# A state-space layer with a routed feed-forward on one core: the first chunk's first block spread over partitions by TensorE instead of through DRAM

## What is computed

```python
xn = layernorm(x)                         # over the 256 features
u_inner = xn @ W_in.T + b_in              # 1024 columns: x (512 channels) and z (the gate)
dbc = x @ W_x.T + b_x                     # 16 columns of delta_raw, 16 of B, 16 of C
delta = softplus(delta_raw @ W_dt.T + b_dt)
A = -exp(A_log)                           # 512 channels x 16 states
h = h * exp(delta_t * A) + x_t * delta_t * B_t      # for each token t in turn
y_t = sum over states of h * C_t
out = (y + x * D) * silu(z) @ W_out.T + b_out
```

## Time and profile before

| | before |
|---|---|
| median of 3 runs | 1965.87 us (1964.99 to 1971.97) |
| the profiled execution | 1968.13 us, of which 1966.3 us are the span from first to last instruction |
| VectorE busy | 1823.1 us, 93% of the span |
| GpSimd busy | 1791.7 us, 91% |
| TensorE busy (matmul) | 1628.6 us, 83% |
| ScalarE busy | 1431.6 us, 73% |
| DMA | 234.92 MB, 119 GB/s on average |
| first scan of VectorE starts | 59.62 us |

### The profile page before, as it was taken

One profiled execution on the slowest core, in us unless ns is written; L12 is line 12 of the kernel. 1 busy time (PEld: TensorE's weight loads), 2 busy tenths in 40 slices (PEclk: granted clock), 3 DMA queues, 4 the chain that ended last, 5 costly groups with the idle time before them and its releaser, 6 DMA issues.

```text
span 1966.3 us, 25727 instructions
## 1 busy us (share of the span) xinstructions
PE 1628.6 (83%) x6816; PEld 808.6 (41%) x6816; DVE 1823.1 (93%) x2246; ACT 1431.6 (73%) x2755; POOL 1791.7 (91%) x780
## 2 busy tenths in 40 slices
PE   3364779898898989889898988889898898988899
PEld 1111224444443444444344444444444444444456
DVE  2799999999999999999999999999999999999951
ACT  3566767877787777878777787877778787777643
POOL 1899999999999999999999999999999999999920
PEclk8666879999899999989999999999999999999999
DMA  4646553544646365464636536463643646265200
GB/s 167 142 112 155 119 138 90 142 123 92 161 111 155 91 152 123 96 151 112 161 84 149 126 92 152 112 165 79 158 118 94 148 111 166 68 156 118 58 14 19
DMA packets 146761, 234.92 MB, mean 119 GB/s; under 512 B 22064, under 2 KB 46896, under 8 KB 146096
## 3 DMA queue, kind: packets, MB, share of 16 engines
q1 hardware_dynamic: 146608, 233.18, 48.7%
HBM read 190.11 MB, written 42.99 MB: 119 GB/s over the span
## 4 chain that ended last, share of the span: by engine, by line
DVE 32%; POOL 23%; issue 17%; PE 17%; ACT 5%; DMA 1%; DVEq 0%; SPq 0%; POOLq 0%; ACTq 0%
POOL hs L1344 14%; DVE decay L1286 13%; DVE hs L1276 8%; DVE hs L1286 7%; POOL hs L1356 6%; PE bank L910 4%; PE bank L932 4%; ACT decay L1089 2%; PE y_ps L946 2%; POOL e_dt L1334 1%; DVE st L1146 1%; POOL z_dt L1323 1%; PE bank L894 1%; PE bank L914 1%; PE bank L884 1%
## 5 line engine op out<-in xcount | busy, mean ns | idle before, releaser
L1344 POOL TENSOR_TENSOR hs<-dx_rep,b_rep 128x2048 f32<-128x2048 f32 x256 | 1161.8, 4541 | 13.4 <-issue 11.1
L1286 DVE TENSOR_TENSOR_SCAN decay<-decay,state,hs 128x512 f32<-128x512 f32 x640 | 796.2, 1277 | 34.2 <-ACT decay L1089 27.4
L1089 ACT ACTIVATE decay<-dt_rep,a_sb 128x512 f32<-128x512 f32 x1024 | 690.0, 685 | 28.7 <-DMA dt_rep<-rep_scratch 10.3
L1286 DVE TENSOR_TENSOR_SCAN hs<-decay,state,hs 128x512 f32<-128x512 f32 x384 | 487.3, 1269 | 4.3 <-ACT decay L1089 3.7
L1356 POOL TENSOR_TENSOR hs<-hs,c_rep 128x1024 f32<-128x1024 f32 x192 | 453.6, 2362 | 6.3 <-ACT state L1103 6.3
L1276 DVE TENSOR_TENSOR hs<-decay,c_rep 128x1024 f32<-128x1024 f32 x320 | 385.1, 1204 | 0.0
L946 PE MATMUL y_ps<-hs,nsum 128*32 128x512 f32 x2048 | 290.3, 641 | 48.8 <-POOL hs L1356 30.6
L910 PE MATMUL bank<-w_i_sb,x_t 128*128 128x512 f32 x484 | 273.5, 693 | 28.9 <-DVE silu L1174 25.5
L868 PE MATMUL bank<-xn_t,w_in_sb 128*128 128x512 f32 x512 | 258.5, 635 | 14.5 <-ACT x_t L996 4.9
L1103 ACT COPY state<-decay 128x2 f32<-128x2 f32 x320 | 51.0, 159 | 266.8 <-DVE hs L1276 260.1
L932 PE MATMUL bank<-w_o_sb,r_t 128*128 128x256 f32 x944 | 224.1, 392 | 2.6 <-ACT r_t L1074 1.8
(11 more groups left out here) (163 smaller groups left out, 1747.7 us busy)
## 6 DMA issues: line engine op xcount, KB each, us to landing
dx_rep<-rep_scratch SPq DMA_DIRECT2D x256, 256.0 KB, 4.7
dt_rep<-rep_scratch SPq DMA_DIRECT2D x256, 256.0 KB, 7.6
b_rep<-bc_scratch SPq DMA_DIRECT2D x256, 64.0 KB, 3.9
rep_scratch<-z_dt SPq DMA_DIRECT2D x64, 256.0 KB, 2.5
rep_scratch<-e_dt SPq DMA_DIRECT2D x64, 256.0 KB, 2.7
c_rep<-bc_scratch SPq DMA_DIRECT2D x256, 64.0 KB, 2.6
xin<-in_u SPq DMA_DIRECT2D x16, 512.0 KB, 4.2
xr<-in_u SPq DMA_DIRECT2D x16, 512.0 KB, 4.3
```

Of the source, the lines that this page charges most:

```text
L1089: nc.scalar.activation(decay[:, j, :], dt_rep[m % 2][:, j, :], ACT.Exp, scale=a_sb[:, J * s + j:J * s + j + 1]).then_inc(decay_ready, 1)
L1286: v.tensor_tensor_scan(hs[s % 4][:, j, :] if kept else decay[:, j, :], decay[:, j, :], hs[s % 4][:, j, :], state[:, b, n:n + 1], ALU.mult, ...
L1344: nc.gpsimd.tensor_tensor(hs[s % 4][:], dx_rep[m % 2][:], b_rep[:, k, :].unsqueeze(1).to_broadcast([P, J, T]), ALU.mult).then_inc(input_re ...
```

## The change

Nothing is changed from chunk 0's second block on. For its first block, and in the prologue:

1. TensorE spreads `e_dt` and `z_dt` of block 0: 4 matmuls for each of 4 tiles j, for each of the two, into `decay` (PSUM), each with 32 columns of the identity as its weights and 32 output partitions. ScalarE copies the first four tiles to `dt_rep[0]`, VectorE the other four to `dx_rep[0]`.
2. The Exp and Ln of the first two blocks are done one block at a time (`first_block` on ScalarE), and V and U of both on VectorE (`first_step`), which also makes the first product with B, in halves; GpSimd only counts it as done.
3. TensorE multiplies zeros: 14 matmuls of 256 columns from the start, and 4 more behind D 1.
4. ScalarE makes the inverse root ahead of A; `rates` (Exp and multiplication of `a_sb`) stands behind the copies.
5. SP no longer loads block 0 back; it issues four groups of B and C ahead of the store, and stores block 1 ahead of block 0.
6. VectorE's work on the later loads stands ahead of job C's part.

```diff
+FIRST = dict(SIDE, pool=[[[x for x in part if x not in ("V0 pre", "U0 pre")] for part in row] for row in SIDE["pool"]])
...
-                for i in range(2):
+                for i in (1, 0) if isinstance(c, int) and c == 0 and pair == 0 else range(2):
                     for kind, src in ((1, z_dt), (0, e_dt)):
                         sp.dma_start(rep_dram[kind, 2 * pair + i], src[:, i, :]).then_inc(rep_stored[2 * pair + i], 16)
...
+                if "main" not in parts and "pre" in parts:
+
+                    waits((bc_stored, 32))
+                    for which, k in ((0, 0), (0, 1), (1, 0), (0, 2)):
+                        load_bc(which, k)
+                    store_rep(0, 0)
+                    for which, k in ((0, 3), (1, 1), (1, 2)):
+                        load_bc(which, k)
...
+            def warm(turns):
+
+                for _ in range(turns):
+                    pe.matmul(y_ps[:, 0:256], state[:].rearrange("p b n -> p (b n)")[:, 0:P],
+                              state[:].rearrange("p b n -> p (b n)"), start=True, stop=True)
+
+            def spread_first():
+
+                for kind, ready, src in ((0, first_delta, e_dt), (1, first_dx, z_dt)):
+                    pe.wait_ge(ready, 1)
+                    for j in range(J):
+                        if kind == 1:
+                            pe.wait_ge(dt_loaded[0], 16 * (j + 1))
+                        for n in range(4):
+                            mm = pe.matmul(decay[32 * n:32 * n + 32, j, :], ident[:, 32 * j:32 * j + 32], src[:, 0, :],
+                                           start=True, stop=True)
+                        mm.then_inc(first_filled, 1)
+
+            pe.wait_ge(zeroed, 1)
+            warm(WARM)
             wait_first(pe)
...
+                    if isinstance(c, int) and c < 0 and i == 1:
+                        mm.then_inc(filled[b], 1)
+                        warm(4)
+                        spread_first()
+                        return
...
-            wait_first(act)
-            nc.scalar.activation(a_sb[:], a_sb[:], ACT.Exp).then_inc(a_ready, 1)
-            act.wait_ge(a_ready, 1)
-            nc.scalar.mul(a_sb[:], a_sb[:], -1.0).then_inc(a_ready, 1)
-            act.wait_ge(a_ready, 2)
+            def rates():
+
+                nc.scalar.activation(a_sb[:], a_sb[:], ACT.Exp).then_inc(a_ready, 1)
+                act.wait_ge(a_ready, 1)
+                nc.scalar.mul(a_sb[:], a_sb[:], -1.0).then_inc(a_ready, 1)
+                act.wait_ge(a_ready, 2)
+
+            def first_block():
+
+                wait_read(act, -1, "pre", "D", (0,))
+                nc.scalar.activation(e_dt[:, 0, :], e_dt[:, 0, :], ACT.Exp, scale=-1.0).then_inc(first_exp, 1)
+                act.wait_ge(first_exp, 1)
+                nc.scalar.activation(e_dt[:, 0, :], e_dt[:, 0, :], ACT.Ln, bias=1.0).then_inc(first_log, 1)
+
+            def keep_first():
+
+                for j in range(J):
+                    act.wait_ge(first_filled, j + 1)
+                    nc.scalar.copy(dt_rep[0][:, j, :], decay[:, j, :]).then_inc(dt_loaded[0], 16)
...
                     at_least(act, rep_stored[(i + 2) % M], 32 * (q + i // 2))
+                    if isinstance(q, int) and q == 0 and i == 2:
+                        act.wait_ge(first_filled, 2 * J)
...
+            def first_step():
+
+                for m, log, delta, dx in ((0, first_log, first_delta, first_dx), (1, log_dt, delta_ready, dx_ready)):
+                    dve.wait_ge(log, 1)
+                    v.tensor_tensor(e_dt[:, m, :], e_dt[:, m, :], z_dt[:, m, :], ALU.add).then_inc(delta, 1)
+                    dve.wait_ge(delta, 1)
+                    v.tensor_tensor(z_dt[:, m, :], e_dt[:, m, :], x_t[0][:, m, :], ALU.mult).then_inc(dx, 1)
+                dve.wait_ge(b_loaded[0], 64)
+                for h in range(2):
+                    for j in (2 * h, 2 * h + 1):
+                        dve.wait_ge(first_filled, J + j + 1)
+                        v.tensor_copy(dx_rep[0][:, j, :], decay[:, j, :]).then_inc(dx_loaded[0], 16)
+                    dve.wait_ge(dx_loaded[0], 32 * (h + 1))
+                    v.tensor_tensor(hs[0][:, 2 * h:2 * h + 2, :], dx_rep[0][:, 2 * h:2 * h + 2, :],
+                                    b_rep[:, 0, :].unsqueeze(1).to_broadcast([P, 2, T]), ALU.mult).then_inc(first_input, 1)
...
                 if "main" not in parts and "pre" in parts:
                     pool.wait_ge(weights_split, 3)
-                    times_b(0, par, 0)
+                    pool.wait_ge(first_input, 2)
+                    pool.sem_inc(input_ready, 1)
```

More of the change, by code:

```diff
@@ L376, in tables @@
         return LAST if c == NC - 1 else END
-    return SIDE
+    return FIRST if isinstance(c, int) and c < 0 else SIDE
 def parts_of(c):
@@ L593, in block_program @@
         weights_ready = sem("weights_ready")
+        first_exp, first_log, first_delta, first_dx, first_filled, first_input = (sem(n) for n in (
+            "first_exp", "first_log", "first_delta", "first_dx", "first_filled", "first_input"))
+        WARM = 14
         NEWTON_STEPS = 5
@@ L803, in body @@
                         load_rep(c + 1, 0)
-                    if "pre" in parts and s >= 12:
+                    if "main" in parts and "pre" in parts and s >= 12:
                         if s == 12:
@@ L988, in job_act @@
                 if letter == "A":
+                    if i == 0 and isinstance(c, int) and c < 0:
+                        wait_first(act)
                     ps, free = wait_filled(act, job[:2], c, when)
@@ L1008, in job_act @@
                     nc.scalar.activation(e_dt[:, i % 2, :], ps[:], ACT.Abs, bias=b_dt_sb[:, i:i + 1]).then_inc(free, 1)
+                    if isinstance(q, int) and q == 0 and i == 0:
+                        first_block()
                 elif letter == "L":
                     wait_read(act, c, when, "D", (2 * i, 2 * i + 1))
-                    nc.scalar.activation(e_dt[:], e_dt[:], ACT.Exp, scale=-1.0).then_inc(exp_dt, 1)
+                    both = slice(1 if isinstance(q, int) and q == 0 and i == 0 else 0, 2)
+                    nc.scalar.activation(e_dt[:, both, :], e_dt[:, both, :], ACT.Exp, scale=-1.0).then_inc(exp_dt, 1)
                 elif letter == "M":
                     act.wait_ge(exp_dt, 2 * q + i + 1)
-                    nc.scalar.activation(e_dt[:], e_dt[:], ACT.Ln, bias=1.0).then_inc(log_dt, 1)
+                    both = slice(1 if isinstance(q, int) and q == 0 and i == 0 else 0, 2)
+                    nc.scalar.activation(e_dt[:, both, :], e_dt[:, both, :], ACT.Ln, bias=1.0).then_inc(log_dt, 1)
+                    if isinstance(q, int) and q == 0 and i == 0:
+                        keep_first()
+                        rates()
                 elif letter == "E":
@@ L1086, in body @@
                                 act.wait_ge(dt_loaded[m % 2], 128 * c + 64 * (m // 2 + 1))
+                            if isinstance(c, int) and c == 0 and s == 0:
+                                act.wait_ge(dx_loaded[0], 16 * (j + 1))
                             if j in (0, 2):
@@ L1279, in scan @@
             def scan(c, b, s, j):
-                if j == 0:
+                if isinstance(c, int) and c == 0 and s == 0:
+                    if j in (0, 2):
+                        dve.wait_ge(first_input, 1 + j // 2)
+                elif j == 0:
                     dve.wait_ge(input_ready, STEPS * c + s + 1)
@@ L1306, in body @@
                 if "main" not in parts and "pre" in parts:
[L1307 to L1310 removed]
+                    first_step()
             sweep(dve, body)
@@ L1338, in times_b @@
                 m, k = divmod(s, KG)
-                if k == 0:
+                if k == 0 or (isinstance(c, int) and c == 0 and s == 1):
                     pool.wait_ge(dx_loaded[m % 2], 128 * c + 64 * (m // 2 + 1))
```

13 lines of the change are left out of this document (6 added, 7 removed).

## The result

| | before | changed |
|---|---|---|
| median, first comparison (4 runs each) | 1965.43 us | 1946.16 us (1945.13 to 1948.0) |
| ratio | 1 | 0.9896 [0.9873, 0.992] |
| median, same kernel measured again in five rounds | 1965.37 us | 1950.44 us (1946.21 to 1951.44) |
| ratio | 1 | 0.9915 [0.99, 0.993] |
| the profiled execution of the first comparison | 1968.13 us | 1945.13 us, span 1942.9 us |

The change makes the kernel 0.9 to 1.0% faster. So the direction and the mechanism can be checked step by step, and there are two things to explain: the sizes, and why one kernel gave two numbers.

What follows compares the result with a forecast made beforehand. An uncovered prologue up to GpSimd's product of step 1 bounds the gain: 4.75 us (root and clock) + 25.4 - 15.2 (D to step 1) = 15.0 us, from median 1965.87 to 1950.9 us; range 1945.5 to 1956.5.

Steps and rivals of the forecast that it cites:

- What bounds: Chunk 0: GpSimd sets the pace from its product of step 1 at 59.79 us; everything before is an uncovered prologue.
- Root ahead of rates: Prologue: the root starts at 7.06 instead of 10.71, 3.65 us earlier; transposes at 11.6; rates cost nothing.
- The clock in B: TensorE's job B: low for some 3 us in place of 5.3, gaining about 1.1 us of a possible 2.65.
- Zeros: TensorE's 14 zero matmuls at the start: end at 10.0 us, before the transposes, or 13.2 if they never raise the clock.
- rival A: TensorE's clock does not follow: zeros don't raise it or it falls between; 4.8 us less, 1955.7; chance 0.09.
- From D to step 1: D's start to GpSimd's product of step 1, spread by TensorE: 15.2 us in place of 25.4.
- ScalarE beside it: ScalarE before the first scan: store lands at d + 12.9, relu of D 2 at d + 13.7, scan at d + 15.8.
- rival B: The store ties up ScalarE: D 2's relu and the scan come 5.2 us later; 5 us less, 1955.9; chance 0.06.
- VectorE's later work moved: VectorE's work on the later loads, ahead of dt_st: ends at 24.2 us or so, costs nothing.
- VectorE's time in hand: Chunk 0: VectorE has 0.89 us in hand, read at 93.52, which covers its lag of 0.7 us.
- Rival C: Chunk 0 gives part back through TensorE's clock: 3 us either side, as 7 us 1958; chance of large loss 0.08.
- Rival D: TensorE's spread: 32 narrow matmuls run one after another, 27 or 54 us in place of 8.5; 1969 to 1997; chance 0.03.

Runs made afterwards that it cites:

- rates first: Changed kernel with ScalarE making the rates ahead of the root again, waiting for the first loads for it; 1953.87 us, ratio 0.9946.
- spread alone: Changed kernel with neither zeros nor the early root, keeping the spread by TensorE, softplus by block and SP's order; 1955.37 us, ratio 0.9953.
- store early: Changed kernel with SP's store behind two groups of B and C loads in place of four; 1949.56 us, ratio 0.9917.
- split copies: Store early, plus ScalarE making copies j = 1 and 2 to dx_rep; GpSimd waits for VectorE's product; 1945.57 us, ratio 0.9901.
- without the 14: Changed kernel without the 14 zero matmuls at the start; 1950.19 us, ratio 0.9925.
- again: The changed kernel measured once more with no edit; 1950.44 us, ratio 0.9915 against the kernel before.
- no zeros: Changed kernel without both groups of zero matmuls, the 14 and the 4; 1953.64 us, ratio 0.9934.
- step 1 free: Store early, with GpSimd's product of step 1 waiting only for the dx_rep copies, not VectorE's products; 1947.24 us, ratio 0.9899.
- shared copies: Step 1 free, plus ScalarE making copies j = 1 and 3 to dx_rep, VectorE's products behind all four; 1952.61 us, ratio 0.9933.
- root alone: Kernel before with the root ahead of the rates and nothing else of the change; 1962.45 us, ratio 0.9985.

## Where the prediction was right, and which step failed

**In short.** I forecast a gain of 15.0 us. The first comparison gives 20.4 by its ratio, the second 16.7. The mechanism held, and the term that failed is the clock in B: root and clock together were put at 4.75 us and gave 7.63. The way from D to step 1 gained 11.3 us, forecast 10.2, with a wrong releaser for ScalarE on it, which gave back 0.8. That makes 18.1 us at chunk 1. The 2.3 us between this and 20.4 are luck: the forecast's 3.0 us of margin allows for such scatter, but no term of the sum stands for it, and no other comparison shows it.

**What bounds: right.** A prologue that no other work covers, with GpSimd's step 1 as its end. It came 18.9 us earlier and 18.1 of it (17.3 and 16.2 in the second run) were there at chunk 1. From step 1 to chunk 1's start it is 108.40 to 108.46 us in eight of the fourteen profiles, before's 108.43 among them, with step 1 anywhere from 40.22 to 59.79. The other six are told below.

**Root ahead of rates: right, a little small.** The root is at 6.95 (forecast 7.1), the transposes at 11.03 (11.6): 4.25 us instead of 3.65. I had kept the 4.57 us between them from the earlier trace rows; it is 4.08 now. The 0.49 us are in three small operations of GpSimd on that way, which took 0.53, 0.25 and 0.31 us before and take 0.20 now. The longest of them, before and after:

```profile
11.50 0.53 POOL L676 TENSOR_TENSOR nw<-nw 128x4 f32<-128x4 f32 x1
```

```profile
7.75 0.20 POOL L682 TENSOR_TENSOR nw<-nw 128x4 f32<-128x4 f32 x1
```

The 0.53 stand in the three profiles with the late root (before, rates first, spread alone), where VectorE splits weights at that time (`w_dt_st`, until 11.97 in before), and in none of the other eleven. Alone the root is worth 3.8 us at chunk 1.

**The clock in B: the mis-sized term.** I forecast that B would be low for some 3 us and gain 1.1 of the possible 2.65, 4.75 us with the root. In the first comparison B was all high, and D came 7.63 us earlier; in the second it was low for 3.4 us as forecast, and D came 5.88 earlier. In the terms of the sum: 1.1 us forecast, 2.60 in B and 0.77 ahead of it measured in the first comparison, 0.90 and 0.77 in the second. Two shares were off: the clock's state itself, which is not fixed by the program (up in five of eight), and the transposes, which I had left at the lower level and which the zeros shortened in seven of the eight, for 0.8 us up to B. My own upper bound for B, 2.65 us, was in the range, but the transposes come on top of it. That the clock stayed up in the first comparison's profile is, by five of eight, about even luck.

The Trainium skill, "TensorE: Matmul & The Clock Gate", Part 4, says that transposes don't count as activity for the clock, by which B would have begun low. The rows differ: in seven of eight profiles the transposes took 1.06 us and B began at the upper level behind them, and in five it stayed there.

**Zeros.** They end at 10.36 (forecast 10.0), before the first transposes; in the nine profiles that have them they end anywhere from 9.07 to 10.58. That zeros raise the clock is shown: with them transposes take 1.06 us in seven profiles, without them 1.94 in all five. So the first half of rival A falls. Its second half, a clock that falls between zeros and B, came in one of the eight (store early, at 11.2), with D at 29.63.

**From D to step 1: 14.13 us, forecast 15.2.** The two things ahead of the spread came as reckoned: Ln ends at D + 3.1 (3.2), TensorE starts at D + 3.9 (4.0), the add takes 0.69 (0.67). The eight tiles take 7.2 us in all (30.65 to 37.80), 0.9 each. I had 8.5, and 0.8 for the clock: 1.3 and 0.8 too much. The row I took (1.06 us for the state sums in the earlier trace rows) is one set by itself; in a chain sets follow each other every 0.9 us, and the clock was at its upper level but for the first 0.2 us. The last part was longer than I thought: from the last tile to GpSimd 3.1 us, not 1.9. VectorE's four copies and two products are 5.2 us on one engine, and they had no gap from 35.40 to 40.63: VectorE, not TensorE, ended the spread. With ScalarE's two copies in between (split copies) step 1 came at D + 13.40.

The Trainium skill, "TensorE: Matmul & The Clock Gate", Part 3, gives 2.38 for three column tiles side by side; an estimate by it puts four at 1.43 us. At 0.9 for four, against 0.89 for one of B's full matmuls at the upper level (7.13 over eight), the row decides.

**ScalarE beside it: this step failed in its releaser.** I had the store landed at D + 12.9 and TensorE ending ScalarE's wait, with 0.8 us to spare. The last issue was at D + 11.15 (forecast D + 10.5) and it took 3.1 us (2.36), so it landed at D + 14.2 and the relu waited for it. In the changed kernel the chain that ended last runs, from D to the first scan, through the issues of SP's sixteen loads and then this store (start, length, what):

```profile
37.88 3.07 DMA rep_scratch<-e_dt
```

The scan was at D + 16.24 (15.8). This is rival B in a small form: it costs 1.0 us, not 5.

**VectorE's later work moved: right.** It ended at 24.15 (forecast 24.2), 1.7 us before VectorE's part of job C began at 25.83, and cost nothing.

**VectorE's time in hand: there, but read in the wrong place, and the lag was larger than reckoned.** I took its wait at 93.52 in the earlier trace rows, 0.89 us, for slack. But GpSimd, too, depends on VectorE within chunk 0, and much earlier. A row of the changed kernel's timeline, where GpSimd waits for VectorE's statistics:

```profile
46.15 0.20 POOL L669 TENSOR_TENSOR ve<-mv,consts 128x4 f32<-128x4 f32 x1 [0.78 <-DVE mv L1217]
```

So what VectorE lags behind GpSimd beyond some point comes back as a wait of GpSimd. The profiles say where the point is. The first scan came 2.02, 2.11, 2.38 and 2.66 us after step 1 (without the 14, changed, again, rates first), and GpSimd waited 0.69, 0.78, 1.05 and 1.33 us: each time the lag less 1.33 us. Up to a lag of 1.07 us (no zeros) it waited for nothing. So VectorE had 1.33 us in hand there, more than my 0.89, and the lag of 0.7 that I reckoned with would have cost nothing. It was 2.11 because of the store. From step 1 to chunk 1 these four take 109.14 to 109.83 us; the other two profiles off the 108.4 are step 1 free (109.33) and shared copies (113.66), where the products of the two engines met. Of the 11.3 us gained between D and step 1, 10.5 are left at chunk 1; in store early, where VectorE lags nothing, 11.4 are.

**Rival C** was right that something scatters and wrong in its place. In chunk 0 nothing more than the 0.8 us is lost. The scatter is in the chunks behind it, 1792.5 to 1798.1 us for the same code, and it accounts for 4.4 of the 6.3 us between the two profiled executions of the changed kernel. What makes it is open; I didn't try to find it. **Rival D** fell: four narrow matmuls take the time of one.

## What to carry to other kernels

A prologue that no work covers is worth as much as its last anchor moves, so follow each step to the instruction that starts the steady pace, and then look, for both engines of the steady part, for the first wait on each other: slack is what is in hand there, and not at a later wait. Warming a clock pays only if the real work follows soon (zeros and an early root were worth more together than apart: rates first lost 5.4 to 7.2 us where the root alone gains 3.8), and the result still varies from run to run. Where the products of two engines exclude each other, an earlier start of one is not a gain: let the product that is wanted first run alone.

## What was not expected of the hardware

A product of VectorE with two SBUF inputs and one of GpSimd exclude each other for the whole of an instruction, by all rows in which they met. VectorE's took 5.5 us in place of 1.2 while GpSimd's ran, GpSimd's 5.4 in place of 4.5 when it started 0.2 us into VectorE's. The Trainium skill, "Advanced Engine Details and Errata", section "GPSIMD Details", says that GpSimd shares a read and a write interface with VectorE and conflicts with VectorE instructions that have two SBUF inputs. The rows agree, and show that the one that comes second waits for the end of the other. In split copies, where no two of them met, all had their own lengths.

The granted clock went either way on the same instructions ahead of B: 1.00 through B in five profiles, 0.50 for some 3.4 us of it in two, and 0.50 from the transposes on in one. In the three that fell, B took 8.83, 8.83 and 9.29 us in place of 7.13.
